# Moving two layer-norm scalings from GpSimd to ScalarE in a fused Mamba, feed-forward and expert kernel

## The chip, the cores and the metric

The kernel runs on one NeuronCore of a Trainium2 chip, everything in float32. The metric is the device time of one execution in microseconds (us); the figure given for a kernel is the median of several runs.

## The reference

The input is x, 2 sequences of 2048 tokens with 256 features. The layer computes, with LN a layer norm without weights:

```
x = x + attn(LN(x))          attn(u) = r + FFN(LN(r)*w2 + b2),  r = u + mamba(LN(u)*w1 + b1)
x = x + experts(LN(x))       8 low-rank experts, top 2 of a softmax router on x/|x|
```

The mamba part has 512 inner channels and 16 states each; per state it runs the recurrence h = h*exp(dt*A) + dt*B*x over the tokens and sums h*C over the states. The feed-forward is 256 to 2x512 (gated by silu) and back to 256. An expert is 256 to 128 to 256.

Two of the layer norms matter here: the one of r (in the code x1) ahead of the feed-forward, and the one of the layer's middle result (x2) ahead of the experts. A normalised token is (value - mean) * rstd.

## The kernel before

A **tile** is 256 tokens of one sequence, as 2 blocks (SUB) of 128 tokens on the 128 partitions. There are 8 tiles per sequence and 2 sequences, so 16 tiles, taken in turn from the two sequences. A tile passes four stages: `enter` (load, norm, input projection, convolution), `ready` (step sizes dt, B, C, gate), `main` (the 16 states), `back` (gate, output projection, r, feed-forward) and `tail` (router, experts, store). `drive` writes the software pipeline down once for all engines: an **iteration** has 16 **slots** (s = 0 to 15), one for each state of the tile n that is in `main`, and in each slot every engine also does one piece of `enter`, `ready`, `back` and `tail` of neighbouring tiles. Iterations 2 to 5 pairs stand in a loop on the engines, the others are written out. Every engine works strictly in the order of its own queue, and waits on semaphores.

Work in `main` for state s, in two halves of two channel groups:

- ScalarE makes `bxT` (L795; for five of the states GpSimd does it, L561) and `dA` (L807), three slots ahead.
- TensorE turns `bxT` into `psx` (L1243), one slot ahead. Three banks of `psx` go round, so the fill of (s+2, first half) has to wait until the scan of (s, second half) has read its bank.
- VectorE scans: `h` from `dA` and `psx` (L998), four instructions a state.
- GpSimd multiplies `hC = h * bC` (L577), and TensorE sums it into `psy` (L1262), two slots later.
- ScalarE keeps the last column of `h` as `state` (L814).

Around the change, in slot 7: VectorE had made x1 in slot 6 and its mean and variance `mv[1]`; ScalarE makes `rstd[2]` (`inv_std`, L662 and L664); GpSimd writes `nx = (x1 - mean) * rstd` (L492, two instructions) and then does `hC` of state 7. In slot 8 TensorE transposes `nx` to `psb` (L1110, released by `vn_done`); in slot 9 ScalarE scales that to `nT` (L855), and TensorE multiplies it with `w_ff_sb` (L1117). In slots 8 and 9 of `ready` VectorE computes the rest of a softplus: `sp_l` (L979, 1024 columns, two inputs in SBUF), `sp_e` (L981), `sp_l` (L985, two inputs in SBUF). The order of VectorE in slot 8 is: scan of the first half, cbc, L979, L981, scan of the second half. In slot 8 and 9 ScalarE also copies `sz` (L754) and `BT` (L747) out of PSUM.

In slot 15 the same is done for the experts: `mv[2]` of x2, `rstd[3]`, GpSimd writes `nx` (L492), then `hC` of state 15, and TensorE transposes `nx` in slot 0 of the next iteration.

The last tile has both normalisations on VectorE, and they stay there.

Of the kernel before, what the change touches and what calls it, by code (L numbers as in the profile page):

```python
# [8 lines left out]
P = 128  # L9
T = 256  # L10
SUB = T // P
# [41 lines left out]
def count(per_step, step, k):  # L53

    c, b = step
    value = c * (2 * per_step) + (per_step * b + k)
    return max(value, 0) if isinstance(value, int) else value
# [6 lines left out]
def is_last(step):  # L64
    return isinstance(step[0], int) and step == (NC - 1, B - 1)
# [117 lines left out]
def mamba_moe(nc, x, params, w_in, w_x, w_dt, w_out, w_ff, w_fo, w_a, w_b, w_r, bc_scratch, cw_scratch, out):  # L183
    f32 = mybir.dt.float32
    ALU = mybir.AluOpType
    ACT = mybir.ActivationFunctionType
# [6 lines left out]
    with ctx:  # L193
        def sb(name, shape):
            return ctx.enter_context(nc.sbuf_tensor(name, shape, f32))

        def sem(name):
            return ctx.enter_context(nc.semaphore(name))
# [31 lines left out]
        mv = [sb(f"mv{k}", [P, SUB, 2]) for k in range(3)]  # L230
        lnv = [sb(f"lnv{k}", [P, SUB]) for k in range(4)]
        rstd = [sb(f"rstd{k}", [P, SUB]) for k in range(4)]
        eps2_c = sb("eps2_c", [P, 1])
        pause = sb("pause", [P, 1])

# [22 lines left out]
        x1 = sb("x1", [P, SUB, DM])  # L258
        nx = sb("nx", [P, SUB, DM])
        nT = sb("nT", [P, KM, T])  # L260
        x2 = sb("x2", [P, B, SUB, DM])
# [26 lines left out]
        def pairs(half):  # L288
# [11 lines left out]
        ident_zero, ident_ready, skip_ready = sem("ident_zero"), sem("ident_ready"), sem("skip_ready")  # L300
# [3 lines left out]
        filled_in, filled_dt, filled_back, filled_tail = (sem("filled_in"), sem("filled_dt"), sem("filled_back"),  # L304
                                                          sem("filled_tail"))
        xf_loaded, xb_loaded, xk_copied = sem("xf_loaded"), sem("xb_loaded"), sem("xk_copied")
        stats = [sem(f"stats{k}") for k in range(3)]
        lnv_done = [sem(f"lnv_done{k}") for k in range(4)]
        rstd_done = [sem(f"rstd_done{k}") for k in range(4)]
        xn_done, un_done, uT_done = sem("xn_done"), sem("un_done"), sem("uT_done")  # L310
        halo_kept, edge_made, edge_summed, edge_added = (sem("halo_kept"), sem("edge_made"), sem("edge_summed"),
                                                         sem("edge_added"))
# [11 lines left out]
        x1_done, x1x_done, vn_done, vT_done = sem("x1_done"), sem("x1x_done"), sem("vn_done"), sem("vT_done")  # L324
        gate_done, hg_done = sem("gate_done"), sem("hg_done")
        x2_done, xe_done, eT_done = sem("x2_done"), sem("xe_done"), sem("eT_done")
# [5 lines left out]
        cw_done, cT_done, cw_stored, cbc_loaded = sem("cw_done"), sem("cT_done"), sem("cw_stored"), sem("cbc_loaded")  # L332
# [5 lines left out]
        def pcol(col):  # L338
            return par[:, col:col + 1]
# [8 lines left out]
        def back_fill(name, m):  # L348
            return count(len(BACK_UNITS), m, BACK_UNITS.index(name) + 1)
# [120 lines left out]
        def _(pool):  # L470
# [13 lines left out]
            def value(v):  # L484

                if not isinstance(v, int):
                    pool.compute_val(v)
                return v

            def normalise(k, dst, src, done):  # L490
                for j in range(SUB):
                    last = nc.gpsimd.tensor_scalar(dst[:, j, :], src[:, j, :], mv[k][:, j, 0:1],  # L492
                                                   rstd[k + 1][:, j:j + 1], ALU.subtract, ALU.mult)
                last.then_inc(done, 1)

            def norm_again(m):

                turned, scaled = value(count(len(IN_UNITS), m, 1 - len(IN_UNITS))), value(count(1, m, 1))
                pool.wait_ge(ident_ready, 1)
                pool.wait_ge(filled_in, turned)  # L500
                pool.wait_ge(rstd_done[1], scaled)
                for j in range(SUB):
                    last = nc.gpsimd.tensor_scalar(un[:, j, :], xf[:, j, :], mv[0][:, j, 0:1],
                                                   rstd[1][:, j:j + 1], ALU.subtract, ALU.mult)
                last.then_inc(un_done, 1)
# [73 lines left out]
                                            ALU.mult).then_inc(hc_done, 1)  # L579

            def back(s, m):
                if s == 7 and not is_last(m):
                    weighed, scaled = value(count(1, m, 0)), value(count(1, m, 1))
                    pool.wait_ge(ident_ready, 1)
                    pool.wait_ge(cw_done, weighed)
                    pool.wait_ge(rstd_done[2], scaled)
                    normalise(1, nx, x1, vn_done)
                if s == 11:
                    pool.wait_ge(xb_loaded, count(16, m, 16))
                    pool.wait_ge(x1_done, count(1, m, 1))  # L590
                    nc.gpsimd.tensor_tensor(xb[:, :, :], x1[:, :, :], xb[:, :, :], ALU.add).then_inc(x1x_done, 1)
                if s == 15 and not is_last(m):
                    turned, scaled = value(back_fill("vT", m)), value(count(1, m, 1))
                    pool.wait_ge(ident_ready, 1)
                    pool.wait_ge(filled_back, turned)
                    pool.wait_ge(rstd_done[3], scaled)
                    normalise(2, nx, x2[:, m[1]], xe_done)

            def tail(s, m):
                if s == 0:  # L600
# [47 lines left out]
        def _(act):  # L648
            def use_log_exp():

                nc.scalar.preload_act_table_set("natural_log_exp_and_others")
# [8 lines left out]
            def inv_std(k, var, m):  # L660

                nc.scalar.activation(lnv[k][:, :], var, ACT.Ln, bias=eps_c[:, :]).then_inc(lnv_done[k], 1)  # L662
                act.wait_ge(lnv_done[k], count(1, m, 1))
                return nc.scalar.activation(rstd[k][:, :], lnv[k][:, :], ACT.Exp, scale=-0.5)  # L664

            def first_deviations(m):


                act.wait_ge(stats[0], count(1, m, 1))
                nc.scalar.activation(lnv[0][:, :], mv[0][:, :, 1], ACT.Ln, bias=eps_c[:, :]).then_inc(lnv_done[0], 1)  # L670
                nc.scalar.activation(lnv[1][:, :], mv[0][:, :, 1], ACT.Ln, scale=1.0 + EPS, bias=eps2_c[:, :]
                                     ).then_inc(lnv_done[1], 1)
                act.wait_ge(lnv_done[0], count(1, m, 1))
                nc.scalar.activation(rstd[0][:, :], lnv[0][:, :], ACT.Exp, scale=-0.5).then_inc(rstd_done[0], 1)
                act.wait_ge(lnv_done[1], count(1, m, 1))
                nc.scalar.activation(rstd[1][:, :], lnv[1][:, :], ACT.Exp, scale=-0.5).then_inc(rstd_done[1], 1)
# [134 lines left out]
            def keep_state(s, n):  # L811

                act.wait_ge(scan_done, count(FILLS, n, HALVES * (s + 1)))
                nc.scalar.activation(state[:, n[1], :, s:s + 1], h[:, ring(s), :, T - 1:T], ACT.Copy  # L814
                                     ).then_inc(state_saved, 1)

            def gate(i, m):

                act.wait_ge(filled_back, back_fill(f"G{i}", m))
                nc.scalar.activation(hg[:, 2 * i:2 * i + 2, :], gate_bank(i, m)[:, :, :], ACT.Silu).then_inc(gate_done, 1)  # L820
# [19 lines left out]
            def back(s, m):  # L840
                if s == 0:
                    keep_state(S - 1, m)
                if s in (3, 4):

                    i = s - 3
                    act.wait_ge(filled_back, back_fill(f"YG{i}", m))
                    nc.scalar.activation(yg[:, 2 * i:2 * i + 2, :], (psb, pst)[i][:, :, :], ACT.Copy).then_inc(yg_moved, 1)  # L847
                if s == 7:
                    act.wait_ge(stats[1], count(1, m, 1))
                    inv_std(2, mv[1][:, :, 1], m).then_inc(rstd_done[2], 1)  # L850
                if s == 9:

                    act.wait_ge(filled_back, back_fill("vT", m))
                    for k in range(KM):
                        last = nc.scalar.activation(nT[:, k, :], psb[:, k, :], ACT.Identity, scale=pcol(C_LN2W + k),  # L855
                                                    bias=pcol(C_LN2B + k))
                    last.then_inc(vT_done, 1)
                if s == 10:
                    gate(0, m)
                    if is_last(m):  # L860
                        gate(1, m)
                        use_log_exp()
                if s == 15:
                    act.wait_ge(stats[2], count(1, m, 1))
                    inv_std(3, mv[2][:, :, 1], m).then_inc(rstd_done[3], 1)

            def tail(s, m):
                if s == 1:
# [576 lines left out]
```

## Time and profile before

| | |
|---|---|
| median of 3 runs | 1306.56 us (1304.96 to 1307.46) |
| the profiled execution | 1305.74 us, of which its span is 1304.0 us |
| TensorE busy | 1222.9 us, 94% of the span |
| VectorE busy | 1006.0 us, 77% |
| ScalarE busy | 1037.6 us, 80% |
| GpSimd busy | 1077.8 us, 83% |
| GpSimd L492, the instructions that leave it | 60, 72.8 us |
| VectorE waiting for TensorE psx | 94.8 us |
| GpSimd hC waiting for VectorE h | 75.2 us |

In the rows, PE is TensorE, DVE VectorE, ACT ScalarE, POOL GpSimd. A timeline row gives start, duration, engine, line, operation, output and inputs, shape and count; in square brackets stand the idle time of the engine before it and what ended it. Where instructions follow each other closely the row's duration is that of the whole group.

### The profile page before, as it was taken

Reading aid. Unit: us, or ns where it says so; the run is one execution under the profiler, and the core shown is the slowest. Engines: PE = TensorE matmul, PEld = TensorE weight load, DVE = VectorE, ACT = ScalarE, POOL = GpSimd, SP = SyncE. Lnnn points to the kernel's source line nnn. Section 1 sums busy time; section 2 is a strip of 40 time slices with the busy share of each in tenths; the row PEclk is TensorE's granted clock in tenths of the full one; section 3 lists DMA queues with packets and bytes.
Section 4 is the critical chain, followed back from the end, with each engine's and each line's share of the span. In section 5 each row is a group of like instructions: output and inputs, shape, how many; then the busy total and the mean of one; then the engine's idle time right before and its main releaser. Section 6 shows DMA issues by size and latency. Waiting matters only on the chain.

```text
span 1304.0 us, 24314 instructions
## 1 busy us (share of the span) xinstructions
PE 1222.9 (94%) x7678; PEld 1053.0 (81%) x7678; DVE 1006.0 (77%) x1800; ACT 1037.6 (80%) x2506; POOL 1077.8 (83%) x820
## 2 busy tenths in 40 slices
PE   5678899999999999999999999999999999999988
PEld 3466778888888888888888888888888888887876
DVE  2597978778796977979688796978879796878733
ACT  4889898799787978878798887879889787978521
POOL 2589899898889988888998988899898888889731
PEclk8798999999999999999999999999999999999999
DMA  1411111121121111112111111212111121112010
GB/s 69 178 49 41 50 42 58 42 76 40 49 82 50 59 40 61 56 50 82 51 58 42 51 64 52 82 36 71 42 50 65 50 74 39 68 35 81 18 49 17
DMA packets 29063, 74.02 MB, mean 57 GB/s; under 512 B 3080, under 2 KB 15744, under 8 KB 26496
## 3 DMA queue, kind: packets, MB, share of 16 engines
q1 hardware_dynamic: 28928, 72.35, 16.4%
q8 instruction: 69, 1.13, 0.4%
q14 instruction: 66, 0.54, 0.1%
HBM read 63.56 MB, written 4.58 MB: 52 GB/s over the span
## 4 chain that ended last, share of the span: by engine, by line
PE 63%; DVE 14%; issue 8%; ACT 5%; POOL 4%; DMA 2%; DVEq 0%; ACTq 0%; SPq 0%; POOLq 0%
PE psx L1243 11%; PE psy L1262 10%; PE pst L1123 8%; DVE h L998 7%; PE psb L1123 7%; PE psb L1117 6%; PE psf L1117 5%; PE psf L1211 2%; PE pst L1117 2%; PE psf L1150 2%; DVE acc L971 2%; POOL hC L577 2%; PE psb L1217 2%; PE psf L1161 2%; DMA cbc<-cw_scratch 2%
## 5 line engine op out<-in xcount | busy, mean ns | idle before, releaser
L998 DVE TENSOR_TENSOR_SCAN h<-dA,state,psx 128x256 f32<-128x256 f32 x1024 | 682.7, 727 | 112.5 <-PE psx L1243 94.8
L577 POOL TENSOR_TENSOR hC<-h,bC 128x1024 f32<-128x1024 f32 x256 | 606.1, 2374 | 82.0 <-DVE h L998 75.2
L807 ACT ACTIVATE dA<-dt,neg_a 128x256 f32<-128x256 f32 x1024 | 434.1, 499 | 0.0
L1243 PE MATMUL psx<-ident,bxT 128*128 128x128 f32 x2048 | 307.5, 276 | 28.4 <-DVE h L998 22.7
L1243 PEld LDWEIGHTS psx<-ident,bxT 128*128 128x128 f32 x2048 | 245.4, 143 | 74.7 <-issue 32.3
L795 ACT ACTIVATE bxT<-uTs,BT 128x512 f32<-128x512 f32 x352 | 232.6, 715 | 67.3 <-PE psx L1243 65.7
L1262 PE MATMUL psy<-ident,hC 128*128 128x128 f32 x2048 | 266.0, 273 | 1.4 <-POOL hC L577 1.4
L1262 PEld LDWEIGHTS psy<-ident,hC 128*128 128x128 f32 x2048 | 233.6, 142 | 4.7 <-POOL hC L577 1.7
L561 POOL TENSOR_TENSOR bxT<-uTs,BT 128x1024 f32<-128x1024 f32 x80 | 151.9, 1899 | 11.2 <-PE psx L1243 11.2
L1123 PE MATMUL pst<-w_b_sb,cbc 128*128 128x256 f32 x480 | 110.8, 379 | 0.0
L1123 PEld LDWEIGHTS pst<-w_b_sb,cbc 128*128 128x128 f32 x480 | 90.1, 190 | 11.7
L1117 PE MATMUL psb<-nT,w_ff_sb 128*128 128x256 f32 x376 | 91.7, 387 | 1.2 <-ACT nT L855 1.1
L971 DVE SCALAR_TENSOR_TENSOR acc<-psf,par,acc 128x255 f32<-128x255 f32 (+1 forms) x180 | 73.9, 474 | 22.0 <-ACT halo L703 22.0
L1117 PEld LDWEIGHTS psb<-nT,w_ff_sb 128*128 128x128 f32 x376 | 68.9, 190 | 15.3 <-issue 5.5
L1117 PE MATMUL pst<-eT,w_a_sb 128*128 128x256 f32 x336 | 79.4, 379 | 0.0
L492 POOL TENSOR_SCALAR nx<-x,mv,rstd 128x256 f32<-128x256 f32 x60 | 72.8, 1225 | 0.0
L1117 PEld LDWEIGHTS pst<-eT,w_a_sb 128*128 128x128 f32 x336 | 61.7, 190 | 7.2
L1117 PE MATMUL psf<-uT,w_in_sb 128*128 128x256 f32 x240 | 60.2, 395 | 5.0 <-DVE acc L971 2.9
L1123 PE MATMUL psb<-w_out_sb,yg 128*128 128x256 f32 x256 | 62.0, 385 | 2.0 <-ACT yg L847 2.0
L1123 PE MATMUL psb<-w_fo_sb,yg 128*128 128x256 f32 x256 | 60.4, 379 | 0.0
L814 ACT ACTIVATE state<-h 128x4 f32<-128x4 f32 x256 | 50.5, 203 | 12.0 <-DVE h L998 12.0
L549 POOL TENSOR_TENSOR dt<-dt,sp_l 128x1024 f32<-128x1024 f32 x16 | 37.8, 2361 | 26.8 <-DVE sp_l L985 26.8
(171 smaller groups left out, 1682.1 us busy)
## 6 DMA issues: line engine op xcount, KB each, us to landing
bC<-bc_scratch SPq DMA_DIRECT2D x64, 512.0 KB, 3.8
cbc<-cw_scratch SPq DMA_DIRECT2D x15, 1024.0 KB, 4.7
xf<-in_x SPq DMA_DIRECT2D x16, 256.0 KB, 2.7
xk<-xn SPq DMA_DIRECT2D x16, 256.0 KB, 4.2
xb<-in_x SPq DMA_DIRECT2D x16, 256.0 KB, 4.3
out<-x SPq DMA_DIRECT2D x16, 256.0 KB, 2.2
w_in_sb<-in_w_in SPq DMA_DIRECT2D x1, 1024.0 KB, 5.4
w_ff_sb<-in_w_ff SPq DMA_DIRECT2D x1, 1024.0 KB, 5.7
```

The source lines that it names most:

```text
L492: last = nc.gpsimd.tensor_scalar(dst[:, j, :], src[:, j, :], mv[k][:, j, 0:1], rstd[k + 1][:, j:j + 1], ALU.subtract, ALU.mult)
L561: nc.gpsimd.tensor_tensor(bxT[:, ring(s)], uTs[:, n[1]], BT[:, n[1], :, s:s + 1].to_broadcast([P, SUB, DI]), ALU.mult).then_inc(bxT_pool, 1)
L577: nc.gpsimd.tensor_tensor(hC[:, s % RC], h[:, ring(s)], bC[:, g % RINGG, s % G:s % G + 1, :].to_broadcast([P, NJ, T]), ALU.mult).then_inc( ...
L795: last = nc.scalar.activation(bxT[:, ring(s), j, :], uTs[:, n[1], j, :], ACT.Copy, scale=BT[:, n[1], j, s:s + 1])
L807: last = nc.scalar.activation(dA[:, s % RA, j, :], dt[:, n[1], j, :], ACT.Exp, scale=neg_a[:, j, s:s + 1])
L814: nc.scalar.activation(state[:, n[1], :, s:s + 1], h[:, ring(s), :, T - 1:T], ACT.Copy).then_inc(state_saved, 1)
L971: nc.vector.scalar_tensor_tensor(out=acc[:, j, tap:], in0=x_bank(i, m)[:, j % 2, 0:T - tap], scalar=pcol(C_CONVW + j * TAPS + k), in1=acc[ ...
L998: last = nc.vector.tensor_tensor_scan(h[:, r, j, :], dA[:, s % RA, j, :], psx[bx_bank(fill)][:, k, :], state[:, b, j, s:s + 1], ALU.mult, ...
L1117: last = mm(dst[:, i, :], w[:, k, c:c + P], rhs[:, k, :], start=k == 0, stop=k == kt - 1)
L1123: last = mm(dst[:, j, :], lhs[:, k, j * P:(j + 1) * P], w[:, k, :], start=k == 0, stop=k == kt - 1)
L1243: last = nc.tensor.transpose(psx[bx_bank(fill)][:, k, j * P:(j + 1) * P], bxT[:, ring(s), j, c:c + P], ident[:, :])
L1262: last = mm(psy[j][:, i * P:(i + 1) * P], hC[:, s % RC, i, j * P:(j + 1) * P], ident[:, :], is_transpose=True, start=False, stop=s == S - ...
```

## The change

ScalarE, which computed rstd in slots 7 and 15, now also normalises. It computes value*rstd + shift, where shift = -mean*rstd. For that it adds, in each of the two slots, one instruction for minus = -mean, two for shift (one for each block) and two for `nx`, with a wait of ScalarE on its own semaphores between them. GpSimd's two instructions in each of these slots go, and so do its waits on `rstd_done`, `cw_done` and `filled_back` there. The waits on `cw_done` and `filled_back` are made by ScalarE instead. Nothing moves in the queues of the other engines.

```
# removed from GpSimd
def normalise(k, dst, src, done):
    for j in range(SUB):
        last = nc.gpsimd.tensor_scalar(dst[:, j, :], src[:, j, :], mv[k][:, j, 0:1],
                                       rstd[k + 1][:, j:j + 1], ALU.subtract, ALU.mult)
    last.then_inc(done, 1)
# back(s, m):
-    if s == 7 and not is_last(m):
-        weighed, scaled = value(count(1, m, 0)), value(count(1, m, 1))
-        pool.wait_ge(ident_ready, 1)
-        pool.wait_ge(cw_done, weighed)
-        pool.wait_ge(rstd_done[2], scaled)
-        normalise(1, nx, x1, vn_done)
-    if s == 15 and not is_last(m):
-        ...
-        normalise(2, nx, x2[:, m[1]], xe_done)

# added to ScalarE
+def mean_shift(k, m):
+    nc.scalar.activation(minus[k][:, :], mv[k][:, :, 0], ACT.Copy, scale=-1.0).then_inc(minus_done[k], 1)
+    act.wait_ge(rstd_done[k + 1], count(1, m, 1))
+    act.wait_ge(minus_done[k], count(1, m, 1))
+    for j in range(SUB):
+        last = nc.scalar.activation(shift[k][:, j:j + 1], minus[k][:, j:j + 1], ACT.Copy,
+                                    scale=rstd[k + 1][:, j:j + 1])
+    last.then_inc(shift_done[k], 1)
+    act.wait_ge(shift_done[k], count(1, m, 1))
+def normalise(k, dst, src, done):
+    for j in range(SUB):
+        last = nc.scalar.activation(dst[:, j, :], src[:, j, :], ACT.Identity, scale=rstd[k + 1][:, j:j + 1],
+                                    bias=shift[k][:, j:j + 1])
+    last.then_inc(done, 1)
 # back(s, m), s == 7, after rstd[2]:
+        if not is_last(m):
+            mean_shift(1, m)
+            act.wait_ge(cw_done, count(1, m, 0))
+            normalise(1, nx, x1, vn_done)
 # back(s, m), s == 15, after rstd[3]:
+        if not is_last(m):
+            mean_shift(2, m)
+            act.wait_ge(filled_back, back_fill("vT", m))
+            normalise(2, nx, x2[:, m[1]], xe_done)
```

## Rows read from the trace of the kernel before

**Rows 1.** Busy time of the engines in two iterations of the steady part
```profile
643.00:720.00 77.00, 75.18 (x482) 65.03 (x481) 62.37 (x111) 63.92 (x156) 67.67 (x52) 1.00 0.17 57
720.00:796.00 76.00, 74.98 (x482) 65.05 (x481) 62.56 (x111) 63.99 (x156) 67.65 (x52) 1.00 0.17 57
```

The columns of Rows 1 are: stretch and length, then the busy us (and instructions) of PE, PEld, DVE, ACT and POOL, TensorE's granted clock as a share of full speed, the DMA share and GB/s.

**Rows 2.** The chain that ended last, slots 7 and 8 of one iteration
```profile
683.80 0.82 DVE sp_l L979
...
687.65 0.72 DVE h L998
```

**Rows 3.** Timeline of GpSimd, slots 7 and 8 of the same iteration
```profile
680.62 2.42 POOL L492 TENSOR_SCALAR nx<-x,mv,rstd 128x256 f32<-128x256 f32 x2
683.01 2.38 POOL L577 TENSOR_TENSOR hC<-h,bC 128x1024 f32<-128x1024 f32 x1
688.61 2.35 POOL L577 TENSOR_TENSOR hC<-h,bC 128x1024 f32<-128x1024 f32 x1 [3.22 <-DVE h L998]
```

**Rows 4.** Timeline of VectorE, the same stretch
```profile
680.65 2.65 DVE L998 TENSOR_TENSOR_SCAN h<-dA,state,psx 128x256 f32<-128x256 f32 x4
...
683.80 2.67 DVE L979 SCALAR_TENSOR_TENSOR sp_l<-sp_l,ln_one,sp_e 128x1024 f32<-128x1024 f32 x1
...
687.00 2.65 DVE L998 TENSOR_TENSOR_SCAN h<-dA,state,psx 128x256 f32<-128x256 f32 x4
...
690.15 1.89 DVE L985 TENSOR_TENSOR sp_l<-sp_l,sp_e 128x1024 f32<-128x1024 f32 x1
```

**Rows 5.** Line L979 over the whole kernel, duration min/median/max in ns
```profile
L979 DVE SCALAR_TENSOR_TENSOR sp_l<-sp_l,ln_one,sp_e x16: 1256/2660/3365, 32.0 to 1137.7; 128x1024 f32<-128x1024 f32 x16
```

**Rows 6.** Timeline of TensorE, slots 8 and 9 of the same iteration
```profile
688.42 0.66 PE L1243 MATMUL psx<-ident,bxT 128*128 128x128 f32 x4 [0.43 <-DVE h L998]
...
689.23 1.99 PE L1117 MATMUL psb<-nT,w_ff_sb 128*128 128x256 f32 x8
```

**Rows 7.** Timeline of TensorE, the same fill of psx in other iterations
```profile
230.39 0.63 PE L1243 MATMUL psx<-ident,bxT 128*128 128x128 f32 x4 [1.21 <-DVE h L998]
...
306.19 0.63 PE L1243 MATMUL psx<-ident,bxT 128*128 128x128 f32 x4 [0.42 <-DVE h L998]
...
1069.35 0.63 PE L1243 MATMUL psx<-ident,bxT 128*128 128x128 f32 x4 [0.43 <-DVE h L998]
...
1142.48 0.63 PE L1243 MATMUL psx<-ident,bxT 128*128 128x128 f32 x4 [0.87 <-DVE h L998]
```

**Rows 8.** Timeline of ScalarE, slot 15 and then slots 7 to 9
```profile
643.62 2.56 ACT L795 ACTIVATE bxT<-uTs,BT 128x512 f32<-128x512 f32 x4 [4.95 <-PE psx L1243]
...
678.78 0.20 ACT L814 ACTIVATE state<-h 128x4 f32<-128x4 f32 x1
...
682.81 0.60 ACT L754 ACTIVATE sz<-psf 128x512 f32<-128x512 f32 x1 [1.02 <-PE psf L1217]
...
686.23 1.00 ACT L855 ACTIVATE nT<-psb,par 128x256 f32<-128x256 f32 x2
689.34 0.20 ACT L747 ACTIVATE BT<-psf 128x32 f32<-128x32 f32 x1 [2.11 <-PE psf L1190]
```

**Rows 9.** Groups of ScalarE instructions by line, nearest to the added ones
```profile
L777 ACT ACTIVATE acc<-xc,par 128x256 f32<-128x256 f32 x64 | 27.1, 494 | 0.0
...
L697 ACT ACTIVATE acc<-psf,par 128x256 f32<-128x256 f32 x60 | 30.6, 562 | 15.7 <-PE psf L1117 15.7
...
L890 ACT ACTIVATE cw<-psel,rden 128x8 f32<-128x8 f32 x30 | 7.4, 299 | 4.5 <-DVE rden L1062 4.5
```

**Rows 10.** Timelines of VectorE, then GpSimd, the first iteration with a normalisation
```profile
150.41 2.65 DVE L998 TENSOR_TENSOR_SCAN h<-dA,state,psx 128x256 f32<-128x256 f32 x4
152.98 1.26 DVE L979 SCALAR_TENSOR_TENSOR sp_l<-sp_l,ln_one,sp_e 128x1024 f32<-128x1024 f32 x1
...
150.88 2.42 POOL L492 TENSOR_SCALAR nx<-x,mv,rstd 128x256 f32<-128x256 f32 x2
153.26 6.12 POOL L577 TENSOR_TENSOR hC<-h,bC 128x1024 f32<-128x1024 f32 x2
```

The columns of Rows 9 are: line, engine, operation, output and inputs, shape and count | busy us, mean ns of one | idle us of the engine before them and what ended it.

More of the change, by code:

```diff
@@ L232, in mamba_moe @@
         rstd = [sb(f"rstd{k}", [P, SUB]) for k in range(4)]
+        minus = {k: sb(f"minus{k}", [P, SUB]) for k in (1, 2)}
+        shift = {k: sb(f"shift{k}", [P, SUB]) for k in (1, 2)}
         eps2_c = sb("eps2_c", [P, 1])
@@ L309, in mamba_moe @@
         rstd_done = [sem(f"rstd_done{k}") for k in range(4)]
+        minus_done = {k: sem(f"minus_done{k}") for k in (1, 2)}
+        shift_done = {k: sem(f"shift_done{k}") for k in (1, 2)}
         xn_done, un_done, uT_done = sem("xn_done"), sem("un_done"), sem("uT_done")
@@ L488, in value @@
                 return v
[L490 to L494, printed above, removed]
             def norm_again(m):
@@ L591, in back @@
                     nc.gpsimd.tensor_tensor(xb[:, :, :], x1[:, :, :], xb[:, :, :], ALU.add).then_inc(x1x_done, 1)
-                if s == 15 and not is_last(m):
[L593 to L596, printed above, removed]
-                    normalise(2, nx, x2[:, m[1]], xe_done)
             def tail(s, m):
```

## The prediction

> **What bounds the kernel now.** I read the busy time by stretch first. In the steady part an iteration takes 76 or 77 us and TensorE is busy for 75.0 to 75.2 of them, at full granted clock; GpSimd is busy for 67.7, ScalarE for 64.0, VectorE for 62.5 [rows 1]. So taking work from GpSimd gives nothing by itself: at most the 1 to 2 us of TensorE's idle time in an iteration are there to be won, and only where a change removes the cause of a wait of TensorE. The question is whether one of these waits hangs on the instructions that move.
>
> Then I read the chain that ended last. It runs through TensorE for nearly all of the iteration, but in slots 6 to 8 it runs through VectorE, ending in L979, L981 and the scan that ends at 688.37 [rows 2], and goes back to TensorE at 688.42, where the fill of psx has waited 0.43 us for that scan [rows 6]. This wait is what can be won. L979 is on that chain, and it takes 2.67 us [rows 4], while the same instruction takes 1.26 us at its shortest and 3.37 at its longest [rows 5].
>
> The timelines of GpSimd and VectorE side by side say why. L979 starts at 683.80, while GpSimd's hC of state 7 runs from 683.01 to 685.39, and it ends at 686.47, which is 1.08 us after that hC [rows 3, 4]. L985 starts at 690.15, under the hC that runs from 688.61 to 690.96, and ends at 692.04, again 1.08 us after it [rows 3, 4]. In the first iteration with a normalisation it is the other way round: L979 starts at 152.98, ahead of the hC at 153.26, takes its shortest 1.26 us, and two hC together take 6.12 us instead of some 4.7 (twice 2.36) [rows 3, 10]. So a VectorE instruction with two inputs in SBUF and an hC exclude each other, and the first one holds. The Trainium skill states this too ("SBUF — State Buffer", the section on two separate sides: an exclusive lock for the whole instruction, the first to start has it, the other fully blocks); the trace agrees for hC against L979 and L985. It would let L492 block L979 as well, and there the trace differs: L979 at 152.98 ran at 1.26 us under the last 0.32 us of L492 [rows 10].
>
> **The change part by part.**
>
> GpSimd loses L492, 2.42 us in slot 7 and as much in slot 15 [rows 3]. In slot 7 hC of state 7 follows L492 without idle time. Its own input is the scan of (7, second half), the second instruction of the group of four at 680.65. In such a group the second one ends 1.37 us after the start (687.00 to 688.37 [rows 2, 4]), so at 682.02, and an hC starts 0.24 us after the scan that releases it (688.61 against 688.37 [rows 2, 3]). Without L492 hC of state 7 thus starts at 682.26 and ends at 684.64 instead of 685.39. L979 still starts at 683.80 and is still blocked, but 0.75 us less: it ends at 684.64 + 1.08 = 685.72, and takes 1.9 us. L981 and the scan behind it come 0.75 us earlier, the scan that releases the fill ends at 687.62, and TensorE, which was ready at 688.42 - 0.43 = 687.99, no longer waits. The gain is TensorE's 0.43 us, not 0.75: behind it the next thing late is TensorE itself. L985 keeps its own block, since the hC of state 8 is released by the same scan and moves with it.
>
> How often: ten iterations show this wait with 0.41 to 0.43 us, the first of them at 306.19 and the last at 1069.35 [rows 6, 7], together 4.2. One, at 842, shows none; there I take nothing. In the second iteration the wait is 1.21 us [rows 7], behind the longest L979, 3.37 us [rows 5]; by the same working hC ends 1.4 us earlier, so I take all 1.21. The last, at 1142.48, has 0.87 [rows 7], of which 0.8 is within reach. Sum: 4.2 + 1.2 + 0.8 = 6.2 us.
>
> The first iteration goes the other way in slot 7. The scan of (7, second half) ends at 150.41 + 1.37 = 151.78 [rows 10], so hC can start at 152.02, ahead of L979 at 152.98, and L979 is blocked until 154.38 + 1.08 = 155.46 instead of ending at 154.24: 1.2 us later on a VectorE that is on the chain there. Against it stands slot 15 of that iteration, where GpSimd has no idle time around L492 and its 2.42 us come off; TensorE's small waits afterwards allow 1 to 1.6 us of it. Bounds: a loss of 1.2 and a gain of 1.5. I take nothing.
>
> Elsewhere in slot 15 GpSimd's 2.42 us are worth nothing: the hC of state 15 behind L492 waits for its scan anyway. The nx that is ready earlier is worth nothing either, since TensorE transposes it in its turn and does not wait for it.
>
> ScalarE gains five instructions in each of the two slots. The trace has no such sequence, so I bound it. Minus: 0.20 us, as the equally small state copy [rows 8]. Two shifts with a scale by pointer: at most 0.30 each [rows 9]. Two normalisations of 128x256: 0.494 each as L777, which is from SBUF to SBUF with a scale by pointer, at most 0.562 as L697, which has the bias too but reads PSUM [rows 9]. Three waits on its own results: from nothing to the 0.24 us of a release between engines. That makes 1.8 to 2.65 us; since neighbouring small instructions overlap, I take 1.8. In slot 15 it lies in the 4.95 us in which ScalarE waits for TensorE [rows 8]. In slot 7, 1.02 us are hidden in the wait ahead of sz [rows 8] and 0.8 us remain: sz, bxT, dA and nT come that much later, nT ends at 688.0 instead of 687.23. TensorE takes nT at 689.23 [rows 6], or 688.8 with its gain, so 0.8 us of cover is left. At the upper bound of 2.65 nT ends at 688.85 and the cover is just gone. ScalarE's wait of 2.11 us ahead of BT [rows 8] then swallows the delay, so none is carried into the next slots. bxT and dA are made three slots ahead, over 12 us, and their delay is hidden there. The waits on cw_done and filled_back that ScalarE now makes are for things that ended many slots before. No DMA and no queue of SP is touched.
>
> Sum: 6.2 us less. The profiled execution took 1305.74 us, 0.8 less than the median of the runs; with the same difference, 1299.5 for an execution like it and 1300.4 for the median.
>
> **The rivals.**
>
> *No change* (1306.5). TensorE is 98% busy, and what it wins in slot 8 it could lose at its next wait, if that hung on something that does not move with it. For it: 0.4 us in 76 is small, and other waits of this size exist. Against it: the waits that I found behind it, for a scan in slot 15 and for acc in slot 7, go back to TensorE's own results within the iteration. Chance 0.2. A half of the gain, 1303.4, has 0.12.
>
> *ScalarE becomes the bound* (slower). Mechanism: nT is late in slot 9, and TensorE waits for it at 689.23. It begins when the added sequence takes over 2.65 us and cancels the gain at about 3.1 us. Were it 3.6 us, nT would end at 689.8 and TensorE would lose 0.6 us against now in some 13 iterations, 8 us, hence 1314. For it: ScalarE is in line for three dependent waits, whose length no row shows. Against it: 3.6 us is a third over the upper bound of the rows. Chance 0.1.
>
> *The first iteration pays* (1299). The 2.42 us of slot 15 there come through to 1.5 us and hC is not ahead of L979. Chance 0.08, and it lies in the likeliest one's own range.
>
> The likeliest case, 1300.4, has 0.5; its own range is 1298 to 1303.
>
> **How the numbers follow.** A measurement of this kernel can tell about 0.2%, 2.6 us, from no change, so faster is below 1303.9. The likeliest, the first iteration's variant, and most of the half gain lie there: 0.68. Same: the case of no change and the rest of the half gain, 0.22. Slower: 0.1. The range goes from 1297.5 (the likeliest with 1.5 of the first iteration and a little more) to 1307 (no change and its spread); it leaves out the slower case and little else.
>
> **What the profile would show.** GpSimd's hC of state 7 starts about 1.6 us behind the start of the scan group of slot 7, with idle time before it. L979 has a median near 1.9 us instead of 2.66. The wait of the psx fill in slot 8 for h is gone, or under 0.1 us. nT's rows start about 0.8 us later against sz of before, and no row of L1117 waits for nT. In the first iteration L979 takes about 2.5 us. The prediction is wrong if L979 stays at 2.66 (then hC did not start earlier, or it was not hC that blocked), if TensorE waits for nT or bxT, or if L979 is shorter and the iteration is still 76 to 77 us long.

## The result and the profile after

| | before | after |
|---|---|---|
| median of 4 runs | 1306.79 us (1304.96 to 1307.46) | 1295.90 us (1295.26 to 1296.41) |
| the profiled execution, its span | 1305.74, 1304.0 | 1295.5, 1293.8 |
| busy TensorE, VectorE | 1222.9, 1006.0 | 1216.8, 996.5 |
| busy ScalarE, GpSimd | 1037.6, 1077.8 | 1086.1, 1004.7 |
| GpSimd hC waiting for VectorE h | 75.2 | 137.1 |

The ratio of the times, after to before, is 0.9914, 95% interval 0.9900 to 0.9929: 11 us faster. The forecast was 1300.4 with a range from 1297.5 to 1307.0, so the direction came out, and the size is beyond the range: 10.9 us where 6.2 were expected.

Line numbers moved: L979, L981 and L985 are now L991, L993 and L997; the scan L998 is L1010; hC's L577 is L575; the psx fill L1243 is L1255 and psy's L1262 is L1274; L1117 is L1129; nT's L855 is L863 and the state copy L814 is L818. First, VectorE in slots 7 to 9 of one steady iteration after, which answers to [rows 4]:

```profile
980.25 2.65 DVE L1010 TENSOR_TENSOR_SCAN h<-dA,state,psx 128x256 f32<-128x256 f32 x4
982.81 0.66 DVE L1085 TENSOR_TENSOR cbc<-cbc,psb 128x512 f32<-128x512 f32 x1
983.39 1.76 DVE L991 SCALAR_TENSOR_TENSOR sp_l<-sp_l,ln_one,sp_e 128x1024 f32<-128x1024 f32 x1
985.08 0.68 DVE L993 TENSOR_SCALAR sp_e<-sp_e 128x1024 f32<-128x1024 f32 x1
985.68 2.65 DVE L1010 TENSOR_TENSOR_SCAN h<-dA,state,psx 128x256 f32<-128x256 f32 x4
```

GpSimd in the same stretch, which answers to [rows 3]; the bracket is its idle time and what ended it:

```profile
981.70 2.37 POOL L575 TENSOR_TENSOR hC<-h,bC 128x1024 f32<-128x1024 f32 x1 [1.56 <-DVE h L1010]
987.13 2.36 POOL L575 TENSOR_TENSOR hC<-h,bC 128x1024 f32<-128x1024 f32 x1 [3.06 <-DVE h L1010]
```

hC of state 7 now starts 1.45 us after the start of its scan group, against 2.36 in [rows 3, 4], and has idle time ahead of it. It ends at 984.07, and L991, which started at 983.39, ends 1.08 us later, the same distance as in [rows 3, 4]. Its duration is 1.76 where it was 2.67.

TensorE, the same stretch after, which answers to [rows 6]:

```profile
986.12 0.60 PE L1255 MATMUL psx<-ident,bxT 128*128 128x128 f32 x4
986.55 1.04 PE L1274 MATMUL psy<-ident,hC 128*128 128x128 f32 x8
987.42 0.60 PE L1255 MATMUL psx<-ident,bxT 128*128 128x128 f32 x4
987.96 0.29 PE L1202 MATMUL psf<-ident,bc 16*128 16x16 f32 x2
988.18 1.99 PE L1129 MATMUL psb<-nT,w_ff_sb 128*128 128x256 f32 x8
```

The fill at 987.42 has no bracket: the wait of 0.43 us is gone. ScalarE after, slot 7 and then nT, which answers to [rows 8]:

```profile
978.38 0.20 ACT L650 ACTIVATE rstd<-lnv 128x2 f32<-128x2 f32 x1
978.49 0.19 ACT L655 ACTIVATE minus<-mv 128x2 f32<-128x2 f32 x1
978.77 0.48 ACT L659 ACTIVATE shift<-minus,rstd 128x1 f32<-128x1 f32 x2
979.29 1.09 ACT L666 ACTIVATE nx<-x,shift,rstd 128x256 f32<-128x256 f32 x2
980.28 0.19 ACT L818 ACTIVATE state<-h 128x4 f32<-128x4 f32 x1
...
986.60 1.00 ACT L863 ACTIVATE nT<-psb,par 128x256 f32<-128x256 f32 x2
```

From minus to the state copy it is 1.79 us, the 1.8 that I took. nT starts 6.35 us after the start of the scan group of slot 7, against 5.58 before [rows 4, 8]: 0.8 us later, as forecast. It ends at 987.60, and TensorE takes it at 988.18, so 0.6 us of cover is left.

### The profile page after: what moved, and what is told of

It reads as the page before. It is cut to its first block, busy times and chain, and to the rows that moved or that the text cites. A ratio compares the mean times of both kernels' runs of the same rounds, so it can differ in the third digit from the quotient of the medians.

```text
span 1293.8 us, 24426 instructions
## 1 busy us (share of the span) xinstructions
PE 1216.8 (94%) x7678; PEld 1051.1 (81%) x7678; DVE 996.5 (77%) x1800; ACT 1086.1 (84%) x2656; POOL 1004.7 (78%) x760
## 4 chain that ended last, share of the span: by engine, by line
PE 72%; DVE 9%; ACT 6%; issue 4%; DMA 4%; POOL 1%; DVEq 0%; ACTq 0%; SPq 0%; POOLq 0%
PE psx L1255 13%; PE psy L1274 12%; PE pst L1135 8%; PE psb L1135 7%; PE psb L1129 7%; PE psf L1129 5%; DVE h L1010 4%; PE pst L1129 4%; DMA cbc<-cw_scratch 3%; PE psf L1223 2%; ACT dA L811 2%; PE psb L1229 2%; PE psf L1162 2%; PE psf L1229 2%; DVE acc L983 2%
## 5 line engine op out<-in xcount | busy, mean ns | idle before, releaser
L1010 DVE TENSOR_TENSOR_SCAN h<-dA,state,psx 128x256 f32<-128x256 f32 x1024 | 682.5, 726 | 112.1 <-PE psx L1255 94.7
L575 POOL TENSOR_TENSOR hC<-h,bC 128x1024 f32<-128x1024 f32 x256 | 604.5, 2368 | 143.8 <-DVE h L1010 137.1
L1255 PE MATMUL psx<-ident,bxT 128*128 128x128 f32 x2048 | 307.0, 276 | 21.8 <-DVE h L1010 17.3
L1255 PEld LDWEIGHTS psx<-ident,bxT 128*128 128x128 f32 x2048 | 245.5, 142 | 64.7 <-issue 25.5
L1274 PE MATMUL psy<-ident,hC 128*128 128x128 f32 x2048 | 265.7, 273 | 1.4 <-POOL hC L575 1.4
L1274 PEld LDWEIGHTS psy<-ident,hC 128*128 128x128 f32 x2048 | 233.0, 141 | 4.6 <-POOL hC L575 1.7
L1129 PE MATMUL psb<-nT,w_ff_sb 128*128 128x256 f32 x376 | 91.7, 387 | 1.4 <-ACT nT L863 1.4
L1129 PEld LDWEIGHTS psb<-nT,w_ff_sb 128*128 128x128 f32 x376 | 68.9, 190 | 15.5 <-issue 5.7
L1129 PE MATMUL pst<-eT,w_a_sb 128*128 128x256 f32 x336 | 79.5, 379 | 0.0
L1129 PEld LDWEIGHTS pst<-eT,w_a_sb 128*128 128x128 f32 x336 | 61.7, 190 | 7.2
L1129 PE MATMUL psf<-uT,w_in_sb 128*128 128x256 f32 x240 | 60.2, 395 | 4.1 <-ACT uT L692 2.1
L818 ACT ACTIVATE state<-h 128x4 f32<-128x4 f32 x256 | 50.3, 202 | 8.7 <-DVE h L1010 8.7
L1135 PEld LDWEIGHTS psb<-w_out_sb,yg 128*128 128x128 f32 x256 | 47.2, 190 | 11.7 <-ACT yg L851 5.8
```

The costliest lines, as they stand in the source:

```text
L575: nc.gpsimd.tensor_tensor(hC[:, s % RC], h[:, ring(s)], bC[:, g % RINGG, s % G:s % G + 1, :].to_broadcast([P, NJ, T]), ALU.mult).then_inc( ...
L1010: last = nc.vector.tensor_tensor_scan(h[:, r, j, :], dA[:, s % RA, j, :], psx[bx_bank(fill)][:, k, :], state[:, b, j, s:s + 1], ALU.mult, ...
L1129: last = mm(dst[:, i, :], w[:, k, c:c + P], rhs[:, k, :], start=k == 0, stop=k == kt - 1)
L1135: last = mm(dst[:, j, :], lhs[:, k, j * P:(j + 1) * P], w[:, k, :], start=k == 0, stop=k == kt - 1)
L1255: last = nc.tensor.transpose(psx[bx_bank(fill)][:, k, j * P:(j + 1) * P], bxT[:, ring(s), j, c:c + P], ident[:, :])
L1274: last = mm(psy[j][:, i * P:(i + 1) * P], hC[:, s % RC, i, j * P:(j + 1) * P], ident[:, :], is_transpose=True, start=False, stop=s == S - ...
```

## The experiments

Each was measured beside runs of the kernel before on its own chip; the chips differ from group to group (the kernel before had medians of 1305.87, 1305.88 and 1307.21 us there), so it is the ratio to before that compares. Nothing of the computation is left out in any; four add instructions whose result nobody reads. "Iteration" is the time from the start of L979 (L991) to its next start, in the steady part. The line numbers shift by a few from kernel to kernel; the rows are known by their tiles.

**Slot 7 alone and slot 15 alone.** The rivals to be told apart: does the gain hang on slot 7, on slot 15, or on the load taken from GpSimd wherever it is taken?

```
# slot7_only: the changed kernel, with GpSimd's normalise back in slot 15
+                if s == 15 and not is_last(m):      # GpSimd
+                    ...
+                    normalise(2, nx, x2[:, m[1]], xe_done)
-                        mean_shift(2, m)            # ScalarE
-                        normalise(2, nx, x2[:, m[1]], xe_done)
# slot15_only: the same with slot 7, mean_shift(1, m), x1 and vn_done
```

> Only the normalisation of slot 7 is on ScalarE; slot 15's stays on GpSimd as before. Theory P (the gain comes from the VectorE instruction with two SBUF inputs, L979, being blocked for a shorter time by the hC of state 7): L979 has a median of 1.85 us, the wait of TensorE for h ahead of the psx fill in slot 8 is gone, and nearly all of the gain is there: 1297 us, 9 to 10 below before. Rival L (any load taken from GpSimd counts, wherever it is): half of the gain, 1301 us.

> Only the normalisation of slot 15 is on ScalarE. Theory P: L979 stays at 2.66 us and the wait in slot 8 stays; only the first iteration with a normalisation, where GpSimd has no idle time, gains 0.9 us: 1305.5 to 1306. Rival L: half of the gain, 1301 us.

Measured: slot 7 alone 1297.89 us, ratio 0.9931 (0.9906 to 0.9955); slot 15 alone 1302.99, ratio 0.9981 (0.9965 to 0.9997). By the ratios that is 9.0 us and 2.5 us, and within the intervals they add up to the whole. For slot 7 alone the theory's number came out. For slot 15 alone the time lies between the two expectations, under the theory's 1305.5 and a little over the 1301 of rival L; the iterations tell them apart. Slot 7 alone has the steady iteration of the whole change (75.33 us, from 375.71 to 451.04), slot 15 alone that of the kernel before (75.96 us, from 377.76). What slot 15 gives lies at the two ends. VectorE in the second iteration, slot 15 alone:

```profile
225.91 2.58 DVE L999 SCALAR_TENSOR_TENSOR sp_l<-sp_l,ln_one,sp_e 128x1024 f32<-128x1024 f32 x1
```

and the same instruction in the kernel before, whose longest it is:

```profile
224.98 3.37 DVE L979 SCALAR_TENSOR_TENSOR sp_l<-sp_l,ln_one,sp_e 128x1024 f32<-128x1024 f32 x1
```

From L979 to L979 the first iteration is 70.88 us instead of 72.00 and the second 75.81 instead of 76.59, together 1.9; from the third on the ordinary iterations of both take the same, but for one of slot 15 alone behind a turn of the engines' loop, with 75.34. At the other end, from the last L979 to TensorE's first matmul with eT, it is 146.22 us instead of 146.95. In the forecast the term of slot 15 stood as nothing.

**The order alone.** If the gain comes only from when hC of state 7 runs, then it must be had without moving any work: GpSimd keeps both normalisations, and its hC of state 7 is made to wait until L979 is done.

```
# before_hc_waits: the kernel before, and in GpSimd's main, ahead of hC
+                    if s == 7 and not is_last(n):
+                        pool.wait_ge(sp_first, count(1, following(n), 1))
# L979
-                                                   in1=sp_e[:, :, :], op0=ALU.subtract, op1=ALU.add)
+                                                   in1=sp_e[:, :, :], op0=ALU.subtract, op1=ALU.add).then_inc(sp_first, 1)
# after_hc_waits: the same two edits on the changed kernel
```

> The kernel before, GpSimd normalises as before, but its hC of state 7 also waits until L979 is done. Theory P: L979 takes its free 1.26 us, the scan behind it comes 1.4 us earlier, TensorE's wait in slot 8 is gone, and the time is within 1 us of the version with only slot 7 changed, 1297 us, although no work has left GpSimd and none has been given to ScalarE. Rival L: no gain, or slower, since GpSimd waits more: 1306 to 1309 us.

> The changed kernel, and hC of state 7 also waits until L979 is done. Theory P: L979 goes from 1.85 to 1.28 us, but TensorE no longer waits for the scan behind it, so the time stays at 1296 us, within 0.2%. Rival (the path through VectorE still sets the pace): 0.57 us in 13 iterations, 1289 us.

Measured: before_hc_waits 1298.43 us, ratio 0.9944 (0.9927 to 0.9961). GpSimd and then VectorE of it, slots 7 to 9 of one iteration:

```profile
903.55 2.42 POOL L493 TENSOR_SCALAR nx<-x,mv,rstd 128x256 f32<-128x256 f32 x2
908.24 4.92 POOL L580 TENSOR_TENSOR hC<-h,bC 128x1024 f32<-128x1024 f32 x2 [2.26 <-DVE sp_l L982]
```

```profile
906.73 1.28 DVE L982 SCALAR_TENSOR_TENSOR sp_l<-sp_l,ln_one,sp_e 128x1024 f32<-128x1024 f32 x1
...
911.68 2.56 DVE L988 TENSOR_TENSOR sp_l<-sp_l,sp_e 128x1024 f32<-128x1024 f32 x1
```

GpSimd still spends its 2.42 us on nx, and then idles 2.26 us more. L979 (here L982) is down to 1.28 us, L985 (L988) is held longer in exchange, and the iteration is 75.35 us. GpSimd does all its old work, ScalarE none of the new, and two thirds of the gain is there, within 1 us of slot 7 alone: neither the load nor an earlier nx was the matter. With the same order on the changed kernel L979 has a median of 1.28 us instead of 1.84, and the time is 1296.07, ratio 0.9932 (0.9915 to 0.9949), no better than the change's. So 0.57 us less on VectorE's chain bought nothing: the iteration is 75.33 us with it and without it. Once the wait in slot 8 is gone, the scan behind L979 no longer sets the pace.

**Load put back, ahead of hC and behind it.** Two instructions like L492 on GpSimd that nobody needs, in the changed kernel, in slot 7 ahead of hC or in slot 8 ahead of the next hC.

```
+            def dummy(m):
+                ...
+                for j in range(SUB):
+                    last = nc.gpsimd.tensor_scalar(junk[:, j, :], w_in_sb[:, 0, j * DM:(j + 1) * DM], lift_c[:, :],
+                                            one_c[:, :], ALU.subtract, ALU.mult)
+                last.then_inc(junk_done, 1)
+                if s == 7 and not is_last(m):    # dummy_behind: s == 8
+                    dummy(m)
```

> The changed kernel, with two instructions of the same size on GpSimd in slot 7 where the normalisation was, reading a weight and writing a tile that nobody reads. Theory P: hC of state 7 starts late again, L979 is back at 2.66 us, and all that slot 7 gave is gone: 1305.5 us. Rival L: half of the load is back, 1301 us. A third possibility, that ScalarE's earlier nx is what helps: stays at 1296 us.

> The changed kernel, with the two dummy instructions on GpSimd one slot later, behind hC of state 7 and in its idle time ahead of hC of state 8. The load on GpSimd is that of the run with the dummy ahead. Theory P: if only instructions with two inputs exclude each other, L979 stays at 1.85 us and the gain stays: 1296 to 1298 us. Rival R (the Trainium skill's rule, SBUF - State Buffer, two separate sides: any GpSimd instruction that reads SBUF holds the shared port): the dummy follows hC without a gap, gets ahead of L979 or not, and where it does L979 takes up to 4.2 us, TensorE's wait in slot 8 is back and longer than before, about 1.7 us in 13 iterations: 1315 us.

Measured: ahead of hC 1304.74 us, ratio 0.9984 (0.9968 to 1.0000), which within the intervals is that of slot 15 alone. Its VectorE, GpSimd and TensorE in slots 7 and 8:

```profile
914.62 2.66 DVE L1003 SCALAR_TENSOR_TENSOR sp_l<-sp_l,ln_one,sp_e 128x1024 f32<-128x1024 f32 x1
```

```profile
911.43 2.44 POOL L500 TENSOR_SCALAR junk<-w_in_sb,lift_c,one_c 128x256 f32<-128x256 f32 x2
913.82 2.38 POOL L585 TENSOR_TENSOR hC<-h,bC 128x1024 f32<-128x1024 f32 x1
```

```profile
919.24 0.66 PE L1267 MATMUL psx<-ident,bxT 128*128 128x128 f32 x4 [0.41 <-DVE h L1022]
```

The picture of the kernel before is back, with ScalarE doing the normalisation. Behind hC the time is 1301.99, ratio 0.9974 (0.9963 to 0.9984), and neither expectation holds: the load is not free there, nor does it bring back the wait in slot 8. GpSimd and VectorE of it:

```profile
909.27 2.38 POOL L585 TENSOR_TENSOR hC<-h,bC 128x1024 f32<-128x1024 f32 x1 [1.56 <-DVE h L1022]
911.63 3.91 POOL L500 TENSOR_SCALAR junk<-w_in_sb,lift_c,one_c 128x256 f32<-128x256 f32 x2
915.52 2.36 POOL L585 TENSOR_TENSOR hC<-h,bC 128x1024 f32<-128x1024 f32 x1
```

```profile
910.88 1.85 DVE L1003 SCALAR_TENSOR_TENSOR sp_l<-sp_l,ln_one,sp_e 128x1024 f32<-128x1024 f32 x1
912.65 0.68 DVE L1005 TENSOR_SCALAR sp_e<-sp_e 128x1024 f32<-128x1024 f32 x1
...
916.40 2.56 DVE L1009 TENSOR_TENSOR sp_l<-sp_l,sp_e 128x1024 f32<-128x1024 f32 x1
```

The dummy pair takes 3.91 us instead of the 2.44 that it takes ahead of hC. The first of the two is the longer one, 2.71 us instead of 1.23, and it starts under L979 (here L1003), with L981 (L1005) behind that; hC of state 8 comes behind it and starts at 915.52, 0.9 us after its scan (which ends at 914.62, by the 1.37 us of the prediction), and now it holds L985 (L1009), which takes 2.56. TensorE meets that late softplus 16 us further on, in the fill with u, by its matmuls and then by its weight loads:

```profile
932.15 0.63 PE L1249 MATMUL psf<-ident,sp_l 128*128 128x128 f32 x4 [0.30 <-issue]
```

```profile
932.12 0.42 PEld L1249 LDWEIGHTS psf<-ident,sp_l 128*128 128x128 f32 x4 [0.51 <-issue]
```

The brackets name no releaser ("issue"), and it isn't u, which GpSimd has written by 926.30. The fill also waits for `bc_done`, since ScalarE copies `bc` out of the same bank, and that copy ends at 932.06, just ahead of the first weight load. ScalarE is late because its `xc` waited for `acc`, which stands in GpSimd's queue behind `dt`, and `dt` needs L985. The two rows of ScalarE:

```profile
921.67 1.06 ACT L724 ACTIVATE xc<-acc 128x1024 f32<-128x1024 f32 x1 [0.88 <-POOL acc L549]
...
931.70 0.36 ACT L730 ACTIVATE bc<-psf 32x256 f32<-32x256 f32 x1
```

In the next two iterations the rows of the fill have 0.21 and 0.42, and the iteration is 75.6 to 75.7 us where the changed kernel has 75.2: 0.4 to 0.5 more. before_hc_waits also has L985 at 2.56, but ends it 7.5 us after the start of L979, not 8.1, and has no such wait; `bc` ends 0.08 us ahead of the fill there. The changed kernel ends L985 after 7.2 us in some iterations and 7.4 in the others. So L985 may end between 0.1 and 0.9 us later than there before TensorE waits, and with `bc` 0.08 us ahead of the fill little is left at 7.5.

**ScalarE's slope.** The slower rival needed a price. Two and then four more normalisations of the same shape on ScalarE, between shift and nx in slot 7.

```
+                        for turn in range(1):       # act_plus4: range(2)
+                            ...
+                            for j in range(SUB):
+                                last = nc.scalar.activation(junk[:, j, :], x1[:, j, :], ACT.Identity,
+                                                            scale=rstd[2][:, j:j + 1], bias=shift[1][:, j:j + 1])
+                            last.then_inc(junk_done, 1)
```

> The changed kernel with two more 128x256 instructions on ScalarE in slot 7, ahead of the normalisation: +1.0 us, so that the sequence takes 2.8 us instead of 1.8. They write a tile that nobody reads. In the profile of the changed kernel nT ends 0.7 us before TensorE takes it. Theory P: 0.3 us of wait for nT in 13 iterations, 1300 us. Rival (ScalarE has over 1 us to spare there): 1296 us.

> As the last one with four more instructions: +2.0 us, sequence 3.8 us. Theory P: nT is 1.3 us late in 13 iterations, 17 us more than the changed kernel: 1313 us, slower than before, as the prediction's rival had it for 3.6 us. Rival: ScalarE's idle time ahead of BT and sz hides most of it, below 1303 us.

Measured: 1299.88 us, ratio 0.9959 (0.9945 to 0.9973), and 1316.87, ratio 1.0097 (1.0080 to 1.0114). ScalarE and TensorE of the second:

```profile
915.55 2.22 ACT L863 ACTIVATE junk<-x,shift,rstd 128x256 f32<-128x256 f32 x4
917.67 1.07 ACT L668 ACTIVATE nx<-x,shift,rstd 128x256 f32<-128x256 f32 x2
...
924.97 1.00 ACT L871 ACTIVATE nT<-psb,par 128x256 f32<-128x256 f32 x2
```

```profile
926.02 1.99 PE L1137 MATMUL psb<-nT,w_ff_sb 128*128 128x256 f32 x8 [1.40 <-ACT nT L871]
```

Its steady iterations take 76.7 to 76.9 us instead of 75.2 to 75.3. With one pair they take 75.5 to 75.7, and the same row has 0.28. So of the first pair's 1.1 us some 0.75 is covered, and all of the second pair's is paid, in every iteration: the rival's mechanism is real. TensorE begins to wait for nT 0.6 to 0.75 us beyond what the change adds, and with 2.2 us more the kernel is slower than before.

**A repeat, and a further cut.** One more wait of a psx fill lies in slot 15, 0.33 us in the steady iterations of both kernels. I took it to hang on VectorE's addition to x2, which stands ahead of the scan. late_x2 does it behind the last scan of the slot, in the changed kernel; before_hc_late has it and the order of before_hc_waits in the kernel before, with nothing moved to ScalarE.

```
# in main of VectorE, behind the scan; the addition ahead of it, in the tail of slot 15, goes
+                if fill == FILLS - 1 and kept:
+                    m = kept.pop()
+                    dve.wait_ge(filled_tail, tail_fill("wb", m))
+                    nc.vector.tensor_tensor(x2[:, m[1]], x2[:, m[1]], pst[:, :, :], ALU.add).then_inc(fin_done, 1)
```

> The changed kernel unchanged, once more, for its spread and for a second profile. Theory P: 1296 us, the wait ahead of the psx fill in slot 8 is gone in every iteration; the jumps at the turns of the loop and the 1.6 us at the end of the kernel before, if they are chance, fall elsewhere.

> The changed kernel, and VectorE adds the experts' output to x2 behind the last scan of slot 15, not ahead of it. The next wait of TensorE in each iteration, 0.33 us by the matmul rows and 0.57 by the weight-load rows, hangs on that scan. By the lesson of the first result the weight-load row gives the gain: the scan can start 0.33 us earlier, so 0.3 us in 14 iterations, 1291 to 1292 us. Rival (the add is then late for something else): 1296 us or more.

> The kernel before with both orders changed, hC of state 7 behind L979 and the add to x2 behind the last scan, and all normalisation on GpSimd. If the two gains add up as on the changed kernel: 1298.4 less 4.5, 1294 us.

Measured: the changed kernel again 1296.87, ratio 0.9918 (0.9900 to 0.9936); late_x2 1294.29, ratio 0.9900 (0.9882 to 0.9919); before_hc_late 1295.51, ratio 0.9926 (0.9907 to 0.9944). TensorE's weight loads of that fill in late_x2:

```profile
640.54 0.42 PEld L1267 LDWEIGHTS psx<-ident,bxT 128*128 128x128 f32 x4 [0.41 <-DVE h L1010]
```

and in the changed kernel:

```profile
640.74 0.42 PEld L1255 LDWEIGHTS psx<-ident,bxT 128*128 128x128 f32 x4 [0.56 <-DVE h L1010]
```

Half of the wait in the matmul row went (0.33 to 0.17) and a quarter of that in the weight-load row, and the iteration is 0.14 to 0.16 us shorter, not 0.3: both rows lost what the iteration did, and what holds the rest of this wait these runs don't name. So the 1291 to 1292 us expected of late_x2 didn't come, nor did the rival's 1296 or more, and before_hc_late is above the 1294 that the sum gave. The intervals of the three overlap, so none is shown to beat the changed kernel. What they show is that two changes of order, with the normalisations left on GpSimd, come to the same time, within the intervals, as moving them.

## Why the prediction was right in kind and short in size

**The step that failed** is "The gain is TensorE's 0.43 us, not 0.75". TensorE's wait was indeed what there was to win, so the mechanism held, but the term was mis-sized: the wait was not 0.43 us long. The steady iterations after are 0.62 to 0.66 us shorter: 75.99 became 75.33, 75.82 became 75.20. The weight loads of the kernel before show that size. Here is one of the ten fills, first by its matmul row, which is of the same kind as those in [rows 7], and then by its weight-load row:

```profile
993.54 0.63 PE L1243 MATMUL psx<-ident,bxT 128*128 128x128 f32 x4 [0.43 <-DVE h L998]
```

```profile
993.51 0.42 PEld L1243 LDWEIGHTS psx<-ident,bxT 128*128 128x128 f32 x4 [0.64 <-issue]
```

The bracket of the weight-load row names no releaser here ("issue"); in the iteration of [rows 6] the same row does name the scan, and where the matmul row of the fill at 842 shows nothing, its weight loads do:

```profile
688.42 0.42 PEld L1243 LDWEIGHTS psx<-ident,bxT 128*128 128x128 f32 x4 [0.66 <-DVE h L998]
```

```profile
841.69 0.42 PEld L1243 LDWEIGHTS psx<-ident,bxT 128*128 128x128 f32 x4 [0.35 <-DVE h L998]
```

By the first of these TensorE was ready at 687.76, and not at 687.99. The iteration of the second, in which I took nothing, became 0.36 us shorter (75.68 to 75.32). The matmul row understates the wait because it counts from the end of the group before it, which the profile only models: after, the psy group ends at 987.59 by its row, 0.17 us after the fill behind it has started. By the starts alone: after, the psy group at 986.55 is followed by the fill 0.87 us later, without a wait; before, from the psy group at 992.07 to the fill at 993.54 it was 1.47. The difference is 0.60 us. Three more from the experiments, as matmul row, weight-load row, and lengthening of the iteration: 0.21, 0.42, 0.4 (dummy_behind); 0.28, 0.37, 0.35 (act_plus2); 1.40, 1.50, 1.49 (act_plus4). The weight-load row is the nearer one each time. One iteration goes against it: the one of the fill at 306.19, with 0.42 and 0.63 in the two rows, became only 0.40 us shorter, and 0.55 in the repeat of the changed kernel.

**The count.** From start to start of L979 (L991) the lag of the kernel before can be followed. The counterpart of [rows 5], with the first and the last start of that line:

```profile
L991 DVE SCALAR_TENSOR_TENSOR sp_l<-sp_l,ln_one,sp_e x16: 1285/1843/2329, 31.9 to 1131.0; 128x1024 f32<-128x1024 f32 x16
```

The last one is 6.7 us earlier than in [rows 5], the first 0.1. By iteration, from the first with a normalisation on, the gain is 0.9, 1.4, 0.4, then some 0.65 in the ordinary ones and 0.36 in the one in which I took nothing. In the three in which the engines' loop starts a new turn it is mixed: they took 77.28, 77.01 and 77.59 us before, 77.48, 78.14 and 76.46 after, and 76.85, 76.87 and 76.63 in the repeat of the changed kernel. If 0.65 is taken for these too, the sum is 8.8 by the last L979, and behind it come 1.9 more, since from there to TensorE's first matmul with eT at the end it was 146.95 us before and 145.03 after. That makes 10.7, near the 10.9 of the medians. Beside my 6.2 the terms are: the ten iterations with the wait, 6.2 instead of 4.2, so 2.0 more; slot 15's gain in the first iteration, taken as nothing, 0.9; the second iteration, 1.4 instead of 1.2; the one at 842, 0.4 instead of nothing; and behind the last L979, where the fill at 1142.48 lies, 1.9 instead of 0.8. Of these only the first two have an experiment behind them; the rest is read from the starts of one trace each. The ends vary: in the repeat the last term is 1.5 instead of 1.9, and the first iteration takes 73.20 us after one of 66.17, where the other trace of the changed kernel has 71.14 after 67.92 and the kernel before 72.00 after 67.75.

**What in the profiled pair isn't the change.** The two spans differ by 10.2 us, but 1.6 of it is TensorE's clock near the end. The same 24 matmuls, before:

```profile
1284.67 7.05 PE L1117 MATMUL psx<-eT,w_a_sb 128*128 128x256 f32 x24
```

and after:

```profile
1276.04 5.43 PE L1129 MATMUL psx<-eT,w_a_sb 128*128 128x256 f32 x24
```

The windows over them, before and after, with the granted clock as the third column from the end:

```profile
1280.00:1284.50 4.50, 2.29 (x16) 1.63 (x15) 1.33 (x3) 0.98 (x3) 0.00 (x0) 1.00 0.17 58
1284.50:1287.00 2.50, 2.50 (x9) 2.05 (x9) 0.70 (x4) 0.22 (x1) 0.88 (x2) 0.51 0.03 7
```

```profile
1276.00:1278.00 2.00, 2.00 (x11) 1.79 (x11) 0.70 (x4) 0.22 (x1) 0.52 (x2) 1.00 0.03 8
```

Before, the granted clock was 0.51 (1.2 GHz) for these 2.5 us, after a stretch in which TensorE was busy for 2.29 us of 4.5; after, at the same place, it was 1.00 (2.4 GHz), and TensorE had been busy for the same 2.29 us of the 4.5 ahead of it. The repeat of the changed kernel took 6.96 us there and slot 7 alone 8.32, both at a granted clock of 0.50 for the first 3 us, so it comes and goes with the execution and is no effect of the change.

**Point by point.** That hC of state 7 would start earlier, and L979 be blocked less because of it: right (1.45 us after the scan group, where 1.61 was said; 1.76 to 1.85 us for L979, where 1.9 was said), and before_hc_waits and dummy_ahead show that this and not GpSimd's load is the cause. The wait of the psx fill: gone. The first iteration's L979: 2.33 us, where 2.5 was said, but the loss of 1.2 that went with it isn't in the time of slot 7 alone (72.06 us there, 72.00 before); instead slot 15 came through, 1.1 in slot 15 alone. I had both bounds and took the middle of them. ScalarE's 1.8 us and the cover for nT of 0.8, found as 1.79 and 0.6: right. That no row of L1117 would wait for nT missed once: in the first iteration L1129 at 158.63 waits 0.31 us for it, where L1117 at 158.46 had 0.09 of idle time. The rival of no change is refuted by the medians; that TensorE would lose its gain at the next wait did not happen. The rival of a slower kernel has its mechanism shown by act_plus4; its place and its slope were right, and the change stays 0.6 us short of it. The variant in which the first iteration pays (1299) came nearest, but not by its condition: hC is ahead of L979 there, which the 2.33 us show, and slot 15's part comes through all the same. The range fell short because its lower end was made of the first iteration's term alone; the reading of the wait itself had no bound.

## What to carry to other kernels

Price a wait of TensorE by the starts of its neighbours, or by its weight-load row, not by the idle time of the matmul row: here 0.43 us in the row were 0.62 to 0.66 in the time of most iterations. Where two engines exclude each other for the length of an instruction, look at what starts first: one semaphore that lets the short VectorE instruction go ahead of the long GpSimd one gave 7.3 us of 11 with no work moved. Before work is given to an engine as cover, find the instruction behind it that may be late by the least before TensorE waits; here that was under a microsecond, with ScalarE 84% busy.

## What the runs showed of the hardware

An instruction of GpSimd with one input tile is held by VectorE too: the dummy pair took 3.91 us instead of 2.44 when it started under L979, with L981 behind that (1.1 and 1.7 us from its start to their ends); so it is in 14 of its 15 turns, and the last, with no L979 over it, has 2.44. The other way round it did not show: L979 at 152.98 ran in 1.26 us although L492 was still running [rows 10], and four more traces, those of slot 15 alone, before_hc_waits, dummy_ahead and before_hc_late, have the same with 1.26 to 1.27. The evidence is thin, though: only the last 0.32 to 0.34 us of L492 overlap, and had L979 been held as it is by hC it would have ended 1.08 us after L492, at 154.38, which is only 0.14 later than it did; ends on GpSimd are rough in the profile. The Trainium skill ("SBUF — State Buffer", section "SBUF: two separate sides") has whichever of the two starts first block the other; for VectorE first these rows agree, for L492 first they differ by those 0.14 us.

A chain of small dependent instructions on ScalarE stood close in this kernel: from the start of minus to that of the first shift it is 0.28 us, and from there to nx 0.52, with a semaphore wait at each.
